# New static instruction orders for a deformable-attention block and a group-norm attention block, with the second attention's key copy on ScalarE

## The reference

```
x_ln = layernorm(x);  q = x_ln @ wq + bq
o = gelu(depthwise_conv7x7_stride2(q) + dw_b)         # 8x8 positions
offsets = o through a 1x1 convolution to 2 channels
interp = bilinear_sample(x, tanh(offsets) + grid)     # 64 samples per image
k = v = interp @ wv + bv
att = softmax((q @ mq_w + mq_b) (k @ mk_w + mk_b)^T) (v @ mv_w + mv_b)   # 8 heads of 16
z = att @ mo_w + mo_b + x
x1 = gelu(layernorm(z) @ mlp_w + mlp_b) + z
```

```
xg = groupnorm(x1, 32 groups of 4 channels)           # over pixels and the group, per image
q, k, v = xg @ wq + bq, xg @ wk + bk, xg @ wv + bv
out = softmax(q k^T / sqrt(128)) v @ wo + bo + x1     # 256 x 256 scores per image
```

## Time and profile before

| | us |
|---|---|
| runs | 79.15, 79.20, 80.45; median 79.2 |
| profiled execution | 79.02 |
| its span, first to last instruction | 77.2 |
| busy in the span: PE, PEld | 67.7, 54.0 |
| busy: DVE, ACT, POOL | 48.2, 36.0, 20.0 |

### The profile page before, as it was taken

One profiled execution on the slowest core, in us unless ns is written; L12 is line 12 of the kernel. 1 busy time (PEld: TensorE's weight loads), 2 busy tenths in 40 slices (PEclk: granted clock), 3 DMA queues, 4 the chain that ended last, 5 costly groups with the idle time before them and its releaser, 6 DMA issues.

```text
span 77.2 us, 2036 instructions
## 1 busy us (share of the span) xinstructions
PE 67.7 (88%) x776; PEld 54.0 (70%) x776; DVE 48.2 (62%) x168; ACT 36.0 (47%) x90; POOL 20.0 (26%) x32
## 2 busy tenths in 40 slices
PE   4969699998999999997999898979786999998860
PEld 2327499973787588976988696837666859996740
DVE  0476623207344789749899836579659695868480
ACT  6112395168218478551331897750556048263600
POOL 5008999900000009160045034204200300000000
PEclk9999999999999999999999999999999999999999
DMA  0888970000000000000000000000000000020112
GB/s 7 228 284 126 305 299 14 0 8 0 0 8 0 0 0 4 8 0 0 0 0 0 13 0 0 0 0 0 0 0 0 0 0 0 13 68 8 59 48 88
DMA packets 3051, 3.07 MB, mean 40 GB/s; under 512 B 225, under 2 KB 2657, under 8 KB 3042
## 3 DMA queue, kind: packets, MB, share of 16 engines
q1 hardware_dynamic: 3042, 2.95, 13.0%
HBM read 2.42 MB, written 0.52 MB: 38 GB/s over the span
## 4 chain that ended last, share of the span: by engine, by line
PE 72%; DVE 11%; issue 4%; DMA 4%; ACT 4%; SPq 1%; DVEq 0%
PE bank L851 40%; PE score L851 21%; PE bank L1027 5%; DMA pack_early<-early 4%; DVE s_sub L626 2%; PE bank L1042 1%; PE score L1206 1%; DVE q_conv L533 1%; SPq L262 1%; PE bank L1206 1%; DVE gst L687 1%; DVE x_t L677 1%; DVE smax L619 1%; PE bank L1066 1%; DVE att L642 1%
## 5 line engine op out<-in xcount | busy, mean ns | idle before, releaser
L435 ACT ACTIVATE p_t<-bank 128x512 f32<-128x512 f32 x8 | 4.8, 597 | 7.8 <-PE bank L1027 7.8
L851 PE MATMUL bank<-v_blk,p_t 128*128 128x34 f32 x64 | 7.9, 269 | 0.0
L851 PEld LDWEIGHTS bank<-v_blk,p_t 128*128 128x128 f32 x64 | 7.9, 193 | 0.1
L619 DVE TENSOR_REDUCE smax<-score 128x8 f32<-128x512 f32 x8 | 5.5, 688 | 3.6 <-PE score L851 3.5
L851 PE MATMUL bank<-q_ph,wd 128*32 128x112 f32 (+5 forms) x256 | 6.7, 249 | 0.0
L331 POOL TENSOR_TENSOR zrs<-zve,neg_half 128x2 f32<-128x2 f32 x4 | 2.8, 708 | 14.4 <-DVE zve L662 14.4
L851 PE MATMUL score<-warm 128*128 128x512 bf16 x14 | 5.2, 496 | 1.0 <-POOL warm L284 1.0
L851 PEld LDWEIGHTS bank<-q_ph,wd 128*32 128x32 f32 x256 | 5.5, 109 | 0.5
L318 POOL TENSOR_TENSOR x_res<-x_st,msa_bias 128x1024 f32<-128x1024 f32 x1 | 2.4, 2365 | 13.5 <-DVE bilin L594 13.5
L626 DVE TENSOR_TENSOR s_sub<-score,smax 128x512 f32<-128x512 f32 x8 | 5.5, 682 | 0.1
L295 POOL TENSOR_TENSOR wd<-pack_early 128x512 f32<-128x512 f32 x4 | 4.1, 1046 | 4.3 <-DVE x_hat L556 4.3
(11 more groups left out here) (184 smaller groups left out, 161.4 us busy)
## 6 DMA issues: line engine op xcount, KB each, us to landing
x_st<-x SPq DMA_DIRECT2D x1, 512.0 KB, 6.8
pack_late<-late SPq DMA_DIRECT2D x1, 448.0 KB, 7.4
out<-y SPq DMA_DIRECT2D x3, 128.0 KB, 1.7
pack_fold<-fold SPq DMA_DIRECT2D x1, 320.0 KB, 4.0
pack_mid<-mid SPq DMA_DIRECT2D x1, 258.0 KB, 5.8
x_hw<-x SPq DMA_DIRECT2D x2, 128.0 KB, 2.1
x_hw<-x SPq DMA_DIRECT2D x1, 256.0 KB, 3.0
pack_early<-early SPq DMA_DIRECT2D x1, 184.0 KB, 3.1
```

What stands on the lines that cost most here:

```text
L435: act.activation(p_t[:, i % 2].rearrange("p j q -> p (j q)"), tile_bank(i)[:, :], ACT.Exp).then_inc(s["exp_ok"], 1)
L619: dve.tensor_reduce(smax[:, i % 2].rearrange("p (j e) -> p j e", e=2), scores, AX.X, ALU.max).then_inc(s["smax_ok"], 1)
L851: return pe.matmul(o, l, r_, start=start, stop=stop, **k)
```

## The change

Every engine but POOL and SP gets a new list. Steps that held several operations are cut into smaller ones, so that they can stand apart:

- PE: `project_qk` becomes `project_q` and `project_k`, with their own semaphores; the transposes of normed z leave `z_transpose` for `zhat_transpose`; `key_half` gives up its value matmuls to `values_half`; `residual_bias` gives up its last row to `residual_row`. `fold_second` writes to bank 5 instead of bank 0. The two `keep_warm(1, 2)` are gone.
- The first half's convolution is done in one piece before `move_half(1)`.
- ACT: takes over the copy of the second half's samples, both value copies of the second half, and all four key copies of the second attention (`key_image(b)`, which waits for DVE's copy of the query from the same bank). `exp_image` is called tile by tile.
- DVE: takes over the attention copies of tiles 6 and 7 (`att_copy`); `project_out` becomes `query_out`.
- The squares of the group norm's two sets lie in bank 7 and bank 0 (`dev_bank`).

The core of the diff, with the hunk headers and blank lines left out and eight columns of indentation taken off; of DVE's list the parts that only shuffle the attention loop are left out:

```diff
     h = slice(e * PIX, (e + 1) * PIX)
     eng.wait_ge(s["v_mm"], g + 1)
     eng.wait_ge(s["vones_set"], 1)
-    if g == 1:
+    if g == 1 and e == 1:
         eng.wait_ge(s["k_ok"], 1)
     copy(v_blk[h, 2 * g:2 * g + 2, :, e * HD:(e + 1) * HD].rearrange("p b j d -> p (b j) d"),
          bank[0][h, 0:G * PAIRS * HD].rearrange("p (n d) -> p n d", d=HD)).then_inc(done, 1)
+V_ACT = 3
+ATT_ACT = 6
 def query_image(b):
...
+    def sample_out():
+        act.wait_ge(s["interp_mm"], G)
+        act.copy(sampled[:, G:B, :].rearrange("p b t -> p (b t)"), bank[0][:, 0:G * PIX]).then_inc(s["sampled_a"], 1)
...
+    def key_image(b):
+        act.wait_ge(s["q1_mm"], b + 1)
+        act.wait_ge(s["k1_mm"], b + 1)
+        act.wait_ge(s["q1_ok"], b + 1)
+        act.activation(k1[:, b], bank[3 + b % 2][:, HW:2 * HW], ACT.Identity, bias=cols1[:, 1:2]).then_inc(s["k1_ok"], 1)
...
+    phases_out(0)
+    act.activation(scratch[:, 1:2], eps[:, :], ACT.Gelu)
+    fold_q_out()
+    gelu_half(0)
+    phases_out(1)
+    tanh_half(0)
+    fold_kv_out()
+    abs_half(0)
+    hats_half(0)
+    fold_columns_out()
+    first_query_out()
+    gelu_half(1)
+    value_half(act.copy, act, 1, 0, s["v_odd"])
+    tanh_half(1)
+    act.activation(scratch[:, 2:3], eps[:, :], ACT.Exp)
+    exp_tile(0)
+    abs_half(1)
+    bias_out()
+    hats_half(1)
+    query_out()
+    sample_out()
+    att_tile(0)
+    exp_tile(1)
+    key_out()
+    value_half(act.copy, act, 1, 1, s["v_odd"])
+    value_half(act.copy, act, 0, 1, s["v_odd"])
+    exp_tile(2)
+    fold_out()
+    att_tile(1)
...
+    exp_tile(7)
+    zhat_image(1)
+    att_tile(5)
+    act.activation(scratch[:, 3:4], eps[:, :], ACT.Gelu)
+    zt_image(0)
+    zt_image(1)
+    gelu_image(0)
+    gelu_image(1)
+    zhat_image(2)
+    out_bias_copy()
+    zt_image(2)
+    zt_image(3)
+    gelu_image(2)
+    gelu_image(3)
+    key_image(0)
+    key_image(1)
     value_copy(0)
-    exp_image(0)
+    exp_image(0, [0])
+    exp_image(0, [1])
+    exp_image(1, [0])
+    key_image(2)
+    exp_image(1, [1])
+    probs_image(0, [0])
+    probs_image(0, [1])
+    probs_image(1, [1])
+    key_image(3)
+    exp_image(2, [0])
+    exp_image(2, [1])
+    probs_image(1, [0])
     value_copy(1)
-    probs_image(0)
-    exp_image(1)
     value_copy(2)
-    probs_image(1)
-    exp_image(2)
+    exp_image(3, [0])
+    exp_image(3, [1])
+    probs_image(2, [0])
     value_copy(3)
-    probs_image(2, [0])
-    exp_image(3)
     probs_image(3, [0])
...
-    def project_out(b):
-        dve.wait_ge(s["qk_mm"], b + 1)
+    def query_out(b):
+        dve.wait_ge(s["q1_mm"], b + 1)
+        dve.wait_ge(s["k1_mm"], b + 1)
         dve.wait_ge(s["cols1_ok"], 2)
         dve.tensor_scalar(q1[:, b], bank[3 + b % 2][:, 0:HW], cols1[:, 0:1], C ** -0.5, ALU.add, ALU.mult).then_inc(s["q1_ok"], 1)
...
+    def att_copy(i):
+        dve.wait_ge(s["attt_mm"], i + 1)
+        dve.wait_ge(s["msa_mm"], i - 1)
+        dve.tensor_copy(att_t[:, i % 2], tile_bank(i)[:, ATT_T]).then_inc(s["attt_v"], 1)
...
+    key_block()
+    value_half(dve.tensor_copy, dve, 0, 0, s["v_even"])
     max_tile(0)
     shift_tile(0)
+    columns_apart(1)
+    rows_apart(1)
+    falling_side(1)
+    column_hat(1)
     max_tile(1)
     shift_tile(1)
-    rows_apart(1)
-    sample_weights(1)
     bilinear(1)
+    recip_tile(0)
+    norm_tile(0)
     max_tile(2)
     shift_tile(2)
-    recip_tile(0)
-    norm_tile(0)
-    sample_out(1)
     max_tile(3)
     shift_tile(3)
-    value_half(dve.tensor_copy, dve, 0, 1, s["v_even"])
...
+    z_offset(1)
+    recip_tile(6)
+    norm_tile(6)
     z_stats(4)
+    z_aggr(4)
+    recip_tile(7)
+    norm_tile(7)
     z_tile(5)
-    recip_tile(6)
-    z_aggr(4)
-    norm_tile(6)
+    att_copy(6)
+    att_copy(7)
     z_stats(5)
-    z_offset(1)
     z_aggr(5)
-    recip_tile(7)
     z_var(2)
-    norm_tile(7)
     z_tile(6)
+    z_tile(7)
     z_stats(6)
-    x1_image(0)
-    z_offset(2)
-    gn_stats(0)
-    z_tile(7)
-    gn_aggr(0)
-    x1_image(1)
     z_stats(7)
-    gn_stats(1)
     z_aggr(6)
     z_aggr(7)
+    z_offset(2)
+    z_var(3)
+    x1_image(0)
+    x1_image(1)
+    gn_stats(0)
+    gn_stats(1)
+    gn_aggr(0)
     gn_aggr(1)
-    z_var(3)
+    zhat_image(3)
+    gn_square(0)
     x1_residual(0)
-    gn_square(0)
+    gn_var(0)
+    norm_image(0)
     x1_residual(1)
-    gn_var(0)
-    zhat_image(3)
-    norm_image(0)
     norm_image(1)
     x1_image(2)
+    x1_image(3)
     gn_stats(2)
-    x1_image(3)
     gn_stats(3)
     gn_aggr(2)
     gn_aggr(3)
+    query_out(0)
+    query_out(1)
+    gn_square(1)
     x1_residual(2)
-    gn_square(1)
-    project_out(0)
+    x1_residual(3)
     gn_var(1)
-    project_out(1)
-    x1_residual(3)
-    max_image(0)
     norm_image(2)
     norm_image(3)
+    max_image(0)
     max_image(1)
-    project_out(2)
-    finish_image(0)
+    query_out(2)
+    query_out(3)
     max_image(2)
-    project_out(3)
-    finish_image(1)
+    finish_tile(0, 0)
+    finish_tile(0, 1)
     max_image(3)
     probs_out(dve.tensor_copy, dve, 2, 1)
+    finish_tile(1, 0)
+    finish_tile(1, 1)
+    probs_out(dve.tensor_copy, dve, 3, 1)
     finish_tile(2, 0)
-    probs_out(dve.tensor_copy, dve, 3, 1)
     finish_tile(2, 1)
-    finish_image(3)
+    finish_tile(3, 0)
+    finish_tile(3, 1)
...
+    def residual_row():
+        mm(bank[6][:, 0:C], ones_row[:, :], r("mo_b"), start=False).then_inc(s["msabias_mm"], 1)
...
-        pe.wait_ge(s["tanh_ok"], G)
-        mm(bank[0][:, 0:C], w("wv1T"), w("wo1"))
-        mm(bank[0][:, C:C + 1], w("wq1"), w("gn_beta"))
-        m = mm(bank[0][:, C + 1:C + 2], w("wk1"), w("gn_beta"))
-        m.then_inc(s["fold1_mm"], 1)
+        pe.wait_ge(s["z_ok"], 1)
+        mm(bank[5][:, 0:C], w("wv1T"), w("wo1"))
+        mm(bank[5][:, C:C + 1], w("wq1"), w("gn_beta"))
+        mm(bank[5][:, C + 1:C + 2], w("wk1"), w("gn_beta")).then_inc(s["fold1_mm"], 1)
...
-            pe.wait_ge(s["w_vo_ok"], 1)
-            pe.wait_ge(s["cols1_ok"], 2)
+            pe.wait_ge(s["tanh_ok"], G)
...
             pe.wait_ge(s["qh_ok"], 2)
         if i == 3:
-            pe.wait_ge(s["v_even"], G)
-            pe.wait_ge(s["v_odd"], G)
+            pe.wait_ge(s["v_odd"], V_ACT)
         if i >= 4:
             pe.wait_ge(s["z_ok"], i - 3)
+        if i == 4:
+            pe.wait_ge(s["w_vo_ok"], 1)
+            pe.wait_ge(s["cols1_ok"], 2)
         for j in range(PAIRS):
             m = pe.transpose(tile_bank(i)[:, j * P:(j + 1) * P],
                              s_sub[:, i % 2, 2 * j:2 * j + 2].rearrange("p h q -> p (h q)"), w("ident"))
...
         pe.transpose(tile_bank(i)[:, ATT_T], att[:, i % 2], w("ident")).then_inc(s["attt_mm"], 1)
     def out_project(i):
-        pe.wait_ge(s["attt_ok"], i + 1)
+        pe.wait_ge(*((s["attt_ok"], i + 1) if i < ATT_ACT else (s["attt_v"], i + 1 - ATT_ACT)))
         mm(tile_bank(i)[:, MSA], att_t[:, i % 2], w("mo_w")).then_inc(s["msa_mm"], 1)
     def z_transpose(b):
         elif b == 2:
             pe.wait_ge(s["x1t_ok"], 1)
+        else:
+            pe.wait_ge(s["dev2_ok"], G)
         for t in range(S):
-            pe.transpose(zt_bank(b)[:, HW + t * P:HW + (t + 1) * P], z[:, 2 * b + t], w("ident"))
+            m = pe.transpose(zt_bank(b)[:, HW + t * P:HW + (t + 1) * P], z[:, 2 * b + t], w("ident"))
+        m.then_inc(s["zr_mm"], 1)
+    def zhat_transpose(b):
         if b < 3:
             pe.wait_ge(s["zhat_ok"], 2 * b + 2)
         else:
         mm(bank[3 + b][:, 0:HW], mlp_wg[:, :], z_t[:, 2 * b:2 * b + 2, :].rearrange("c s q -> c (s q)")).then_inc(s["mlp_mm"], 1)
     N = len(SHIFTS)
+    def x1_transpose(b):
+        pe.wait_ge(s["x1t_ok"], b + 1)
...
+    def project_ready(b):
+        pe.wait_ge(s["xgn_ok"], b + 1)
+        pe.wait_ge(s["gamma_ok"], 1)
+        if b < 2:
+            pe.wait_ge(s["x1res_ok"], b + 1)
+        else:
+            pe.wait_ge(s["q1_ok"], b - 1)
+            pe.wait_ge(s["k1_ok"], b - 1)
+    def project_q(b):
+        project_ready(b)
+        mm(bank[3 + b % 2][:, 0:HW], wq1g[:, :], x_gn[:, b]).then_inc(s["q1_mm"], 1)
+    def project_k(b):
+        project_ready(b)
+        mm(bank[3 + b % 2][:, HW:2 * HW], wk1g[:, :], x_gn[:, b]).then_inc(s["k1_mm"], 1)
+    def project_v(b):
+        pe.wait_ge(s["xgn_ok"], b + 1)
...
     conv_half(0, 0, 6)
+    conv_half(0, 6, N)
     move_half(1)
-    conv_half(0, 6, N)
+    coord_half(0)
     fold_keys()
-    coord_half(0)
-    conv_half(1, 0, 5)
+    conv_half(1, 0, 11)
+    sample_half(0)
     query_half(0)
-    sample_half(0)
-    conv_half(1, 5, 8)
     key_half(0)
-    conv_half(1, 8, 12)
+    conv_half(1, 11, 16)
+    values_half(0)
     score_tile(0)
-    conv_half(1, 12, N)
+    coord_half(1)
     residual_bias()
-    coord_half(1)
+    residual_row()
     score_tile(1)
+    transpose_scores(0)
     query_half(1)
-    transpose_scores(0)
+    value_tile(0)
     score_tile(2)
+    sample_half(1)
     transpose_scores(1)
+    att_transpose(0)
```

(114 more changed lines are left out.)

255 lines of the change are left out of this document (115 added, 140 removed).

## The result

The changed kernel takes 72.8 us (median of 4 executions, 72.4 to 73.9), against 79.8 (79.2 to 82.7) for the kernel before on the same chip. The ratio is 0.919, 95% interval 0.912 to 0.925: 6.5 us less on 79.2.

The account below looks back on a forecast made before the run. TensorE was taken as the bound. Five fewer shape changes (1.0 us) and waits down from 9 to 6 us gave 4.1 us, cut for hand-overs to 2.9: 79.2 - 2.9 = 76.3 us, range 74.9 to 78.6.

Parts of the forecast that it names:

- The discount for hand-overs: About ten passages from PE to ACT or DVE, each 0.1 to 0.2 us late, take back 1.0 to 1.3 us.
- The first two rows of the table: Front of the kernel: first-half sampling forecast at 18.55 us (old 19.11), second score tile at 24.0 (old 24.98).
- VectorE at full record durations: Whole new order: VectorE instructions charged their full record lengths, though their starts follow closer; no size given.
- the first rival: Whole kernel: the walk is right as it stands, 75.1 us; chance 0.20.
- the walk: From 11.7 us on: the new order stepped through with the old trace's durations; 4.1 us gained.
- Changes of tile shape: PE from 11.7 us on: 27 changes instead of 32 at 0.2 us each, 1.0 us less work.
- the largest step: MLP of images 2 and 3, moved from between z transposes and projections: last gelu at 53.15 instead of 56.96 us.
- The first half: Convolution to second-half sampling: that sampling at 27.55 us against 29.82, about 1.2 to 1.7 us ahead in work.
- the gain of the front: Convolution to first scores: second score tile at 24.0 against 24.98 us; exp table load hidden with 0.4 to spare.
- their new wait: Second attention: key copy waits for query copy; priced at nothing, but two PE waits of 0.35 us for images 2 and 3.
- The second rival: Last stage: key copies behind exponentials on ACT lose 1.9 of the 2.9 us gained, 78.2 us; chance 0.22.
- the third rival: Group norm: without warm matmuls PE falls to 1.2 GHz, 81.3 us; chance 0.08, shared with an overlooked queue.

Follow-up runs that it names:

- before_morewarm: The kernel before with five more warm matmuls in TensorE's waits of the middle stage; median 79.2 us, undisturbed ratio to the kernel before 1.000.
- shape_together: Changed kernel with five tiny 128x128 matmuls in one place behind tap 10 of the second half's convolution; 72.7 us in one full-clock execution, no ratio.
- front_old: Changed kernel with TensorE's and ScalarE's old order up to the second score tile; ratio 0.946, 2.3 us over the changed kernel.
- keys_dve: Changed kernel with the four key copies back on VectorE, each behind its query copy; ratio 0.932, 73.1 to 73.9 us.
- shape_apart: Changed kernel with five tiny 128x128 matmuls set apart between 32-column taps of the second half's convolution; ratio 0.935.
- dve_extra: Changed kernel with one more small VectorE reciprocal behind each of eight attention norms; ratio 0.922, 72.5 to 72.9 us in three executions, 154.8 in the fourth.
- att_act: Changed kernel with the attention copies of tiles 6 and 7 back on ScalarE, behind its gelu table load; ratio 0.931.
- old_stage3: Changed kernel with the old lists from the second attention's first scores on and keys copied by VectorE; ratio 0.942, 74.0 to 74.6 us.
- before_nowarm: The kernel before without its two warm matmuls at the group norm; median 80.9 us, one of six executions at full clock (79.1).
- old_stage2: Changed kernel with the old lists from the first attention's end to the second group-norm spread; ratio 0.971, 76.4 to 77.0 us at full clock.

## Why the prediction was wrong

The prediction has 2.9 us of gain, the chip 6.5. The 3.6 that are missing are, within 0.1, two terms of the sum.

**The discount for hand-overs, 1.2 us: the step "I do not believe all of it" failed.** The late starts of 0.1 to 0.2 us per hand-over were real where I read them, on the old trace, in a stage in which PE waited at each one. The first two rows of the table, where PE waits for a chain through ScalarE and VectorE, are late by such an amount too (0.2). They seem to be paid only where PE waits. In the new order PE is busy 11.99 of 12.00 in the loop and 13.16 of 14.00 behind it, so most hand-overs lie behind other work of PE. I multiplied by ten a price that the change itself removes. This is argued from the windows; no run measured a hand-over by itself.

**VectorE at full record durations, 2.3 us: the step "DVE was priced with full durations" was the mis-sized one.** I named it for the first rival and kept it in the walk. The loop gives 1.0 of it, and about 0.8 of this lies behind the last score tile, where the walk had PE wait for VectorE. There VectorE's nine instructions ahead of the last subtraction take 1.90 us by their starts and 2.54 by their records, which is 0.64 of the 0.8; PE still waits about 0.2 us for them. Eight further instructions in the loop cost nothing that can be measured (1.5 us of VectorE by full records of 0.19). The 0.9 us between the fourth gelu and the first maximum, where aggregates, residuals and queries queue on VectorE, and the last 0.3 fit the same cause, but no run tested it there.

**Changes of tile shape: 0.2 us for every one was too much, but not for the score tiles.** It is 0.11 between 128x32 and 128x128, and 0.18 to 0.23 at the score tiles, where I had read it. Five fewer are worth 0.6 to 1.1 us, depending on which, and the 1.0 lies within. The walk also charged 0.2 for each of the changes that are left, and where those are narrow ones it came out late by it. Up to the last score tile it was late by at most 0.25 us, so this explains little of the miss; how much is not separated.

**Where the gain lies: right.** The middle stage is the largest, and the MLP order of images 2 and 3 in it (3.0 us by itself) the largest step; the fourth gelu came 4.5 us earlier, where at least 2.5 were asked for. The first half was right to 0.25 us. But I read the gain of the front only in its own slots. Put back by itself half of it costs 2.3 us, of which about 1.2 are traced to the table load that it pushes out of its cover.

**The keys: their new wait was priced at nothing beside two waits of 0.35 us, and the move as a whole gains 1.3 us.** The second rival (the last stage eats the lead) is refuted: the lead is 4.8 us at the second aggregates and 6.4 at the last y, with 0.39 added to both. The new wait of ScalarE on the query copy costs less than VectorE gains by the four copies, as the 1.3 us [0.6, 2.0] say; no run measured the wait by itself.

**The clock: the mechanism of the third rival exists, on the other side.** I wrote that the granted clock of the profile tells nothing of it. For the start of the kernel that holds; in mid-kernel a fall shows as 0.5. It hits the kernel before more often (27 of 53 executions) than the changed one (3 of 12), though this one has two warm matmuls fewer. That the new order has fewer falls because it fills the waits of the middle stage fits `before_morewarm`, but it is not shown: of the kernels with the new middle stage and an edit elsewhere `shape_together` fell in three of four executions, `front_old` and `keys_dve` in one of four each, and `shape_apart`, `dve_extra`, `att_act` and `old_stage3` in none. The evidence that I gave against the rival, an undisturbed wait of 1.28 us in one profile, was one execution of a thing that happens in half of them. The Trainium skill, "TensorE: Matmul & The Clock Gate", on clock oscillation ("A second HAM failure mode: psum-queue depth-cycling"), says that short idle times between groups of matmuls can keep the clock switching. The runs agree, at waits of 0.80 and 0.55 us in `before_nowarm` and 1.05 us in `shape_together`; an execution with a fall took 1.3 to about 4 us more than the undisturbed ones of its kernel.

## What to carry to other kernels

Walk an order with the spacing of starts, not with the lengths of records, and don't discount the walk for hand-overs that lie behind other work of the bound engine. Before crediting or clearing an early edit, look for a table load or another fixed block behind it: in `front_old` a tanh late by 1.43 us came out as 1.15 in every later tile, while the score tile ahead of them was only 0.4 us late. Where executions of one kernel scatter by some per cent, list the granted clock of each, and put a few warm matmuls into the waits of the stage in which it falls.

## What the hardware showed that I had not expected

- TensorE's mean granted clock read under 0.99 in 27 of 53 executions of the kernel before. The kernel before was profiled only without a fall; in the profiles of `before_nowarm`, `old_stage2` and `shape_together` the clock was 0.5 for 3 to 7 us in mid-kernel, in `before_nowarm` behind a microsecond with PE busy 0.44. Executions with a fall took 1.3 to about 4 us more. With five warm matmuls in the waits it fell in none of 12 executions, at no cost (ratio 1.000).
- One execution of `dve_extra` took 154.8 us, with weight-load records about twice as long (433 ns against 192) under a granted clock of full.
- A change between 128x32 and 128x128 tiles costs TensorE 0.11 us, one to the 32x128 score tiles and back 0.18 to 0.23 each way (an estimate).
- VectorE started small instructions 0.11 to 0.12 us apart (37.18, 37.30 and 37.41), though their records last 0.18 to 0.19.
- Stages put back one by one cost 3.1, 4.4 and 2.1 us where the whole change gives 6.5.
